# One block for the relative-position attention stage, three turning banks in a ring, and two results in one PSUM bank

## The reference, cut to what matters

```python
b, s, d = x.shape                       # 4, 512, 128
idx = jnp.arange(s)
dist = jnp.clip(idx[None, :] - idx[:, None], -R, R) + R          # R = 64
pe_k, pe_v = rel_emb_k[dist], rel_emb_v[dist]                    # (s, s, 8)
qkv = jnp.transpose((x @ W_qkv + b_qkv).reshape(b, s, 3, H, hd), (2, 0, 3, 1, 4))
q, k, v = (qkv[0], qkv[1], qkv[2])
q = q / jnp.sqrt(jnp.asarray(hd, x.dtype))
score = jnp.einsum('bhqd,bhkd->bhqk', q, k) + jnp.einsum('bhqd,qkd->bhqk', q, pe_k)
attn = jax.nn.softmax(score, axis=-1)
ctx = jnp.einsum('bhqk,bhkd->bhqd', attn, v) + jnp.einsum('bhqk,qkd->bhqd', attn, pe_v)
return jnp.transpose(ctx, (0, 2, 1, 3)).reshape(b, s, d) @ W_out + b_out
```

## Time and profile before

| | |
|---|---|
| Times of three runs | 1484.61, 1489.88, 1497.74 us; median 1489.88 |
| The profiled execution | 1488.59 us; its span, from the first to the last instruction, 1486.9 us |
| PE busy | 1159.3 us (78%) |
| DVE busy | 839.2 us (56%) |
| ACT busy | 712.7 us (48%) |
| POOL busy | 306.2 us (21%) |
| Mean granted TensorE clock | 0.906 |

### The profile page before, as it was taken

The page is one execution under the profiler, slowest core; times in us unless marked ns, Lnnn a source line. Parts: engine busy times, 40 slices in busy tenths (PEclk is TensorE's granted clock), DMA queues, the critical chain, the costliest instruction groups (busy, mean ns, idle before and its releaser), DMA issues. The chain is left out here.

```text
span 1486.9 us, 35646 instructions
## 1 busy us (share of the span) xinstructions
PE 1159.3 (78%) x14780; PEld 578.3 (39%) x14780; DVE 839.2 (56%) x1359; ACT 712.7 (48%) x1328; POOL 306.2 (21%) x639
## 2 busy tenths in 40 slices
PE   5677677888858997578999999999676655588886
PEld 2222332333233442246666666666443223122221
DVE  3575336777632323237666666666226342799994
ACT  4100443777522223536665665555232332389894
POOL 1443010333202322034223223222002101100000
PEclk9999866999968998689999999999889886699998
DMA  4000006111005320140030030110200000611100
GB/s 163 1 0 0 1 0 213 46 46 46 3 0 115 70 44 0 72 72 4 3 24 4 3 24 3 10 11 3 17 1 0 0 1 1 214 36 47 36 24 30
DMA packets 133665, 51.61 MB, mean 35 GB/s; under 512 B 103113, under 2 KB 125657, under 8 KB 132858
## 3 DMA queue, kind: packets, MB, share of 16 engines
q1 hardware_dynamic: 133506, 49.34, 14.3%
HBM read 33.12 MB, written 15.81 MB: 33 GB/s over the span
## 5 line engine op out<-in xcount | busy, mean ns | idle before, releaser
L1728 DVE TENSOR_REDUCE re_nmax<-ps 128x1 f32<-128x512 f32 x256 | 158.9, 683 | 113.1 <-PE ps L1562 113.1
L1577 PE MATMUL ps<-const,re_p 128*128 128x128 f32 x1024 | 154.8, 284 | 33.0 <-DVE re_pT L1743 26.6
L1695 ACT ACTIVATE re_p<-ps,re_nmax 128x512 f32<-128x512 f32 x256 | 154.5, 693 | 16.2 <-DVE re_nmax L1728 16.2
L850 DVE TENSOR_REDUCE ga_nmax<-ps 128x2 f32<-128x1024 f32 x128 | 147.9, 1217 | 14.3 <-PE ps L656 14.2
L1684 ACT ACTIVATE re_pT<-ps 128x512 f32<-128x512 f32 x128 | 76.6, 598 | 162.0 <-PE ps L1577 162.0
L783 ACT ACTIVATE ga_pt<-ps 128x512 f32<-128x512 f32 x256 | 139.2, 598 | 30.6 <-PE ps L691 28.9
L1577 PEld LDWEIGHTS ps<-const,re_p 128*128 128x128 f32 x1024 | 109.1, 142 | 63.4 <-ACT re_p L1695 47.2
L850 DVE TENSOR_REDUCE da_nmax<-ps 128x2 f32<-128x256 f32 (+3 forms) x128 | 102.3, 822 | 38.3 <-PE ps L667 36.9
L783 ACT ACTIVATE da_pt<-ps 128x512 f32<-128x512 f32 (+3 forms) x256 | 97.5, 438 | 46.6 <-PE ps L691 45.6
L1743 DVE COPY re_pT<-ps 128x512 f32<-128x512 f32 x128 | 82.6, 686 | 22.9 <-PE ps L1577 22.2
L710 PE MATMUL ps<-ga_pt,ga_v 128*9 128x256 f32 x1024 | 81.1, 385 | 9.6 <-ACT ga_osum L796 9.4
(11 more groups left out here) (384 smaller groups left out, 2020.9 us busy)
## 6 DMA issues: line engine op xcount, KB each, us to landing
ex_gates<-gates_scratch SPq DMA_DIRECT2D x4, 2048.0 KB, 14.7
da_stacks<-da_qkparts SPq DMA_DIRECT2D x8, 384.0 KB, 3.1
da_qst<-da_stacks SPq DMA_DIRECT2D x32, 96.0 KB, 2.3
da_kst<-da_stacks SPq DMA_DIRECT2D x32, 96.0 KB, 2.4
ga_stacks<-ga_qkparts SPq DMA_DIRECT2D x8, 384.0 KB, 3.1
ga_qst<-ga_stacks SPq DMA_DIRECT2D x32, 96.0 KB
ga_kst<-ga_stacks SPq DMA_DIRECT2D x32, 96.0 KB
da_stacks<-da_qkparts SPq DMA_DIRECT2D x8, 256.0 KB, 3.1
```

Of the source, the lines that this page charges most:

```text
L850: nc.vector.tensor_reduce(nmax[:, u % 2, :, pr, qt], g.ps[:, score_bank[step]:score_bank[step] + 2, 0:keys_of(qt)], AX.X, ALU.max, negate= ...
L1577: last = nc.tensor.transpose(g.ps[:, T_BANK + tile % 2, bass.ts(kt, 128)], p[:, QUAD_ORDER[idx], bass.ts(kt, 128)], g.c("ident"))
L1695: nc.scalar.activation(p[:, quad, :], g.ps[:, S_BANK + quad, :], ACT.Exp, bias=nmax[:, s % 2, idx:idx + 1]).then_inc(exped, 1)
L1728: nc.vector.tensor_reduce(nmax[:, s % 2, idx:idx + 1], g.ps[:, S_BANK + quad, :], AX.X, ALU.max, negate=True).then_inc(maxed, 1)
```

## The change

- The block of projections and the block of the attention become one. TensorE projects batch by batch and swaps each batch's queries right after it, with banks 0 to 5 for the projections in turns and 6 and 7 for the swaps. SP stores each batch's queries as they come and loads the first two batches back at once. Before its first scores TensorE waits for all of the copies, the tables (`less`), and the bias. The buffers of the projections (`xn`, `q_tok`, `zero`, `raw`) now lie in the second half of `pT`, so engines wait for the stores and the tables before they first write there (step 4).
- The banks for turned tiles are three (4, 5, 6), used as a ring; the pieces of a batch's tail take their turn in the same ring.
- Bank 7 holds the far unit in columns 0 to 127 and the near values in the next 64. ScalarE copies each after every step (`copy_values`, `copy_near`); both groups of matmuls wait for the other's copy. VectorE masks the near values out of SBUF (`near`), one step later than before and behind its copies of tiles.
- TensorE turns all four tiles before the next step's scores. ScalarE takes its four exponentials first, and then copies tiles 2 and 3.
- The far unit runs four steps late; the logarithm of the tail stands between the second and third exponentials, its exponential at the end of the step.
- The near values are stored and fetched back for each group of four steps (a quarter of a batch); for the quarter that ends a batch, the loads of the queries two batches on go ahead of its fetches.

The diff, cut to its core:

```diff
-    FAR_LAG = GS + 1
-    TAIL_LAG = STEPS_B + 2 * GS - 3
-    S_BANK, T_BANK, V_BANK, N_BANK = 0, 4, 6, 7
+    FAR_LAG = GS
+    TAIL_LAG = STEPS_B + GS
+    S_BANK, T_BANK, T_BANKS, V_BANK = 0, 4, 3, 7
...
+        ring = []
+        for step in range(ALL_STEPS):
+            ring += [("tail", phase, tail_batch(step, phase)) for phase in range(3)
+                     if tail_batch(step, phase) is not None]
+            if step < NSTEPS:
+                ring += [("tile", step, idx) for idx in range(4)]
+        slot_of = {entry: n for n, entry in enumerate(ring)}
...
+        def bank_of(*entry):
+            return T_BANK + slot_of[entry] % T_BANKS
...
+        far_out = g.ps[:, V_BANK, 0:128]
+        near_out = g.ps[:, V_BANK, 128:128 + 2 * HD * OCT]
...
+                pe.wait_ge(g.weights_loaded[5], 16)
+                for b in range(B):
+                    project(b)
+                    swap(b)
...
+                pe.wait_ge(copied, 3 * B)
+                pe.wait_ge(bias_added, 1)
+                pe.wait_ge(less, 2 * OCT + 2)
...
+                def wait_ring(slot):
+                    if slot < T_BANKS:
+                        return
+                    what, n, m = ring[slot - T_BANKS]
+                    if what == "tail":
+                        pe.wait_ge((logged, divided, added)[n], m + 1)
+                    elif m < 2:
+                        pe.wait_ge(dve_pT, 2 * n + m + 1)
+                    else:
+                        pe.wait_ge(act_pT, 2 * n + m - 1)
...
                     if s >= 1:
-                        pe.wait_ge(masked, s)
...
+                        pe.wait_ge(near_out_read, s)
...
-                        if n >= 1:
-                            pe.wait_ge(osum_out, n)
+                    pe.wait_ge(near_out_read, min(unit + FAR_LAG - 1, NSTEPS))
+                    if unit >= 1:
+                        pe.wait_ge(osum_out, unit)
...
                 for s in range(ALL_STEPS):
                     if s < NSTEPS:
                         score(s)
-                    if 1 <= s <= NSTEPS:
-                        turn(s - 1, 3)
                     if FAR_LAG <= s < NSTEPS + FAR_LAG:
                         far_unit(s - FAR_LAG)
                     if 1 <= s <= NSTEPS:
                         near_values(s - 1)
+                    tail(s)
                     if s < NSTEPS:
-                        for idx in range(3):
+                        for idx in range(4):
                             turn(s, idx)
-                    tail(s)
...
+                def copy_near(s):
+                    if s >= 2:
+                        act.wait_ge(o_done, s - 1)
+                    nc.scalar.activation(near[:, s % 2, :], near_out, ACT.Identity).then_inc(near_out_read, 1)
...
+                def copy_values(unit):
+                    n, quad = divmod(unit, GS)
+                    b, qt = divmod(n, QT)
+                    act.wait_ge(far_done, unit + 1)
+                    if b >= 2 and unit % STEPS_B == 0:
+                        act.wait_ge(joined, b - 1)
+                    nc.scalar.activation(osum[:, b % 2, quad, bass.ts(qt, 128)], far_out, ACT.Identity)\
+                        .then_inc(osum_out, 1)
...
                 for s in range(ALL_STEPS):
-                    if 1 <= s <= NSTEPS:
-                        evacuate(s - 1, 3)
                     if s < NSTEPS:
...
+                        exponentials(s, 0)
+                        exponentials(s, 1)
...
+                        nc.scalar.activation(inverse[:, :], g.ps[:, bank_of("tail", 0, b), :], ACT.Ln)\
+                            .then_inc(logged, 1)
+                    if s < NSTEPS:
+                        exponentials(s, 2)
+                        exponentials(s, 3)
+                        evacuate(s, 2)
+                        evacuate(s, 3)
+                    if 1 <= s <= NSTEPS:
+                        act.wait_ge(near_done, s)
+                    if FAR_LAG <= s < NSTEPS + FAR_LAG:
+                        copy_values(s - FAR_LAG)
+                    if 1 <= s <= NSTEPS:
+                        copy_near(s - 1)
...
                 for b in range(B):
...
+                    sp.wait_ge(q_out, b + 1)
+                    sp.dma_start(q_dram[b * T:(b + 1) * T, :].rearrange("(t p) c -> p t c", p=128),
+                                 q_tok[:, b, :, :]).then_inc(q_stored, 16)
+                    if b < 2:
+                        sp.wait_ge(q_stored, 16 * (b + 1))
+                        load_queries(b)
+                sp.wait_ge(q_stored, 16 * B)
+                for n in range(GROUPS):
+                    b, qt = divmod(n, QT)
+                    sp.wait_ge(o_done, GS * (n + 1))
+                    octets = slice(16 * qt, 16 * qt + 16)
+                    sp.dma_start(o_dram[b, octets].rearrange("a p d -> p a d"), o[:, b % 2, octets, :])\
+                        .then_inc(o_stored, 16)
+                    sp.wait_ge(o_stored, 16 * (n + 1))
+                    if qt == QT - 1 and b + 2 < B:
+                        load_queries(b + 2)
...
+                    for two in range(2):
+                        sp.dma_start(ot[64 * two:64 * two + 64, qt, :].rearrange("p (h d) -> p h d", d=HD),
+                                     rows[two]).then_inc(ot_loaded, 16)
```

More of the change, by code:

```diff
@@ L1500, in far_values @@
                             .then_inc(far_ready, 1)
+                nc.gpsimd.memset(ends[:, :, :], 0.0).then_inc(set_up, 1)
+                nc.gpsimd.memset(v9[:, :, :, HD:HD + 1], 1.0).then_inc(set_up, 1)
+                nc.gpsimd.memset(zero, 0.0).then_inc(set_up, 1)
+                pool.wait_ge(copied, 2)
                 set_keys(0)
@@ L1654, in tail @@
                         pe.wait_ge(divided, b + 1)
-                        pe.wait_ge(masked, min(step, NSTEPS))
-                        nc.tensor.matmul(g.ps[:, N_BANK, :], g.w("aout"), oT[:, :], start=True, stop=True)\
-                            .then_inc(made, 1)
+                        wait_ring(slot_of["tail", 2, b])
+                        nc.tensor.matmul(g.ps[:, bank_of("tail", 2, b), :], g.w("aout"), oT[:, :], start=True,
+                                         stop=True).then_inc(made, 1)
                 for s in range(ALL_STEPS):
@@ L1679, in free_pT, with exponentials @@
                         act.wait_ge(near_done, GS * (n - 1))
+                def exponentials(s, idx):
+                    act.wait_ge(maxed, 4 * s + idx + 1)
+                    if s >= 1:
+                        act.wait_ge(turned, 4 * (s - 1) + idx + 1)
+                    nc.scalar.activation(p[:, QUAD_ORDER[idx], :], g.ps[:, S_BANK + QUAD_ORDER[idx], :], ACT.Exp,
+                                         bias=nmax[:, s % 2, idx:idx + 1]).then_inc(exped, 1)
                 def evacuate(s, idx):
@@ new lines, in _ @@
+                table = ins["rel_v"]
+                for to, n, at in ((0, 128, T - 128), (128, 64, T - 256 + 64), (192, 64, T)):
+                    overlapping = bass.AP(table.tensor, at * HD, [[HD, 128], [1, n * HD]])
+                    sp.dma_start(rel_v[:, to:to + n, :].rearrange("p s d -> p (s d)"), overlapping)\
+                        .then_inc(v_table, 16)
+                sp.wait_ge(set_up, 1)
+                for n, row in ((0, 0), (1, table.shape[0] - 1)):
+                    one_row = bass.AP(table.tensor, row * HD, [[0, 128], [1, HD]])
+                    sp.dma_start(ends[:, n, 0:HD], one_row).then_inc(ends_loaded, 16)
```

331 lines of the change are left out of this document (140 added, 191 removed).

## The result

| | before | after |
|---|---|---|
| Median of 4 runs each | 1489.29 us (1484.61 to 1497.74) | 1440.79 us (1439.25 to 1450.89) |
| Ratio, 95% interval | | 0.968 (0.962 to 0.975) |
| Way in | 36.30 | 25.84 |
| Loop, 62 periods | 386.67 | 362.93 |
| Way out | 30.90 | 18.58 |

The last four lines are cut as in the prediction: from the start of the block to the second step's first row maximum, on to the last step's first maximum, and to the end of the addition to x. The forecast was 1443 us in a range of 1430 to 1466. The three parts give 46.5 us of gain against 46.9 booked. The profiled execution of after is the longest of its four (1450.89); outside the stage, where nothing was changed, it lost 8.8 us against that of before (1488.59 - 1450.89 = 37.7, and 46.5 - 37.7 = 8.8). Its mean granted clock was 0.904, that of the other three 0.915 to 0.917.

A forecast was written before the change was run, and what follows sets the result against it. TensorE, busy 91% of the loop, idles mostly on VectorE's copies. Savings of 10.8 (way in), 25.7 (loop), 0 (tails) and 10.4 us (way out) sum to 46.9: 1488.6 becomes 1441.7, as median 1443 us, range 1430 to 1466.

The forecast's parts named there:

- Way in: Stage start to second step's first row maximum: early query load brings second maximum to 652.0, saving 10.8 us, bounds 7 and 12.
- Way out: Last step's maxima to stage end: quarter stores and fetches cut 30.9 to 20.5 us, saving 10.4, bounds 7 and 12.5.
- The third bank removes the wait before the third tile: Middle loop steps: 0.51 us of TensorE idle before the third tile goes, saving 0.45 us a step.
- TensorE becomes the bound: Middle loop steps: TensorE's own work, 5.69 us, exceeds the waits' 5.50, so the step falls from 6.14 to 5.69.
- the loop of waits: Loop: scores to maxima 1.64, maxima through first tile's copy 3.3, last tile 0.56, together 5.50 us in a middle step.
- the 5.6 to 5.8 that were to show it right: Loop: sign that the forecast holds, middle periods between 5.6 and 5.8 us.
- The first rival: Loop: the fourth tile takes the place of the wait it frees, step stays 6.14 us; 1469 us, chance 0.12.
- Edge steps: Loop steps near a batch's ends: the waits decide, 5.72 falls to 5.41 us, saving 0.31 in each of 16.
- Tails at 0: Three pieces ending each batch, in the ring of three: at most +0.4 x 3 = 1.2 us against free banks, booked 0.
- Shared bank: Far and near values in one bank: no cost, 0.28 us of cover; as second rival, late copies give 1459 us, chance 0.12.
- no cold restart: Way in: the first period becomes 5.4 us, with TensorE not restarting cold.
- The clock: Third rival, loop: TensorE granted 1.2 GHz, middle step roughly 10.2 us, half the loop gives 1583 us; chance 0.04.

The follow-up runs named there:

- The square: Kernel after with two or three banks, four tiles ahead of the scores or fourth behind: loops 400.0 and 388.4 us (two banks), 362.9 and 354.4 (three).
- the late load: Against the kernel after, the first two batches' queries loaded only after all four stores, still in one block: 1451.66 us.

## Why the prediction was right, and where its steps were off

**The third bank removes the wait before the third tile, the masking multiply no longer matters.** Right, and the largest term. The square shows 34 to 37 us for it, more than the 25.7 booked for the loop, because another part takes some back. The multiply costs next to nothing in middle steps; ahead of the copies it would cost 0.07 us in an edge step.

**"TensorE becomes the bound", at 5.69 us.** This step failed in its working. The prediction added up two sums, TensorE's list (5.63, taken as 5.69) and the loop of waits that starts at the maxima (5.50), took the larger, and left no wait. The middle step is neither sum but a path that crosses from one to the other. TensorE's groups ahead of the tiles take 3.33 us (812.99 to 816.32); the copy of the first tile starts 0.79 after that tile does and takes 0.69; 0.12 later comes the fourth tile's weight load, and 0.59 later the next scores: together 5.52. The prediction did name this wait ("only the fourth waits for the first tile's copy"), but let the copy start when the maxima end, where it starts when the first tile is ready, and so found no idle time in it.

The list itself was too long. Three tiles in a row take 811.74 - 810.23 = 1.51 us, where 0.56 each makes 1.68: a tile takes 0.56 only as the last before the scores. So the old wait before the third tile was 0.70 us rather than 0.51, and 6.14 - 0.70 = 5.44, the period of the old order with three banks. In the order of the kernel after the list is about 5.28 (an estimate: 3.33, 1.51, and 0.44 for one more tile between two others, as the trace of the old order has it), and some 0.24 of wait make up the rest.

That the forecast of 5.69 lies near the measured 5.52 to 5.59 is in part luck, and the middle periods lie outside the 5.6 to 5.8 that were to show it right. The total for the loop (23.7 against 25.7) hides this. Middle steps gained 0.6 each instead of 0.45, which with the edge steps would make 46 x 0.6 + 16 x 0.31 = 32.6 us. The tails (2.1) and the gaps that no engine released (5.3 more than before, see below) were not booked and took most of the difference back. Two errors of about 7 us cancelled: that is luck.

**The order of tiles.** The first rival put the fourth tile between the last exponential and the next scores, held by "the same copy of the first tile", and gave it 0.12 for the whole gain. The wait for that copy is there, at a third of the size: the order costs 8.5 us of loop. A middle step takes 5.54 instead of 5.44, some 4.6 us in 46 steps, and the gaps without a releaser are 4 us more than in the old order. I had taken four tiles ahead for a part of the gain; the square shows that it is a loss in either column of banks. It is hidden because the third bank's gain is four times as large.

**Edge steps.** 5.41 booked, 5.38 to 5.50 measured, and most of them are decided as booked, by the loop of maxima and exponentials.

**Tails at 0.** Nearly so: the three long steps after the first batch took 7.14, 8.23 and 7.0 us before and take 6.79, 7.90 and 6.58 now, 1.1 less together, while three ordinary steps gained 1.8. Measured so, a tail costs 0.7 more than it did beyond its steps.

**Shared bank.** Right that it costs nothing. The far copy takes 0.27 us (0.28 booked) and the near copy 0.23, and they overlap, so they end at 0.99 instead of 1.27. The cover is 0.65 us where I had 0.28, and the two runs with more copies lie on either side of its end. The Trainium skill's advice in "Perfetto Trace Analysis", section "Matmuls", to rotate independent groups of matmuls through different banks is thus a question of slack here: with one more copy of 0.38 us the step kept its length, and with 1.21 us of them the far unit waited 0.45 us in most middle steps.

**Way in.** 10.8 booked, 10.5 measured in one execution and 9.0 in the other. The chain was right: the loads decide (the late load gives all of it back), and they arrived at 646.37, or 645.3 with this block's later start (1.05 us) taken off, where 644.7 was expected (the 646 that was to show it wrong did not reckon with the later start). What I had ruled out, "no cold restart", happens in the second execution: queries come 0.43 us after TensorE could use them, the clock falls, and the first four tiles take 3.60 us instead of 2.39. It is the more common case: of seven executions with this way in, two took 25.8 us and kept the clock, five took 27.2 to 27.4 and lost it (the same kernel again and four with edits elsewhere).

**Way out.** 10.4 booked, 12.3 measured. The store of a quarter takes 3.0 us where I took 4.1, and from the join to the end 4.9 instead of 6.1, with the clock at 1.00: the wait for the fetches is now 0.73 us, not 10.7, and the output's two matmuls take 1.12 us, not 2.08. The Trainium skill has a rule for DMAs that GpSimd issues ("DMA: Bandwidth & Descriptors", section "Anatomy of one DMA": about 2.0 us and the bytes over 436 GB/s); for 64 KB it would make 2.2 us, an estimate from that page. These stores are issued by SyncE, in 32-byte pieces, and took 3.0 us for a quarter and 9.2 for a whole batch, so they neither bear the rule out nor refute it.

**The clock.** Right: 1.00 through 362.9 us of denser work.

**What I had not booked.** Gaps inside the near values, released by no engine. The profile sums them to 2.5 us in the loop of before, but 2.2 of these are something else: one of 0.73 us in each of three steps at the start, which stands ahead of the group and not in it:

```profile
669.28 0.60 ACT L1684 ACTIVATE re_pT<-ps 128x512 f32<-128x512 f32 x1 [1.69 <-PE ps L1577]
...
669.98 0.45 PE L1602 MATMUL ps<-re_rel_v,re_pT 128*32 128x16 f32 x32 [0.73 <-issue]
```

There no far unit stands between yet, and near values begin 0.10 us after the end of ScalarE's copy of the fourth tile (669.88), for which they wait; in the step before these three the profile itself names that copy. That leaves 0.3 us before, against 5.6 after and 5.3 when run again. Such a step:

```profile
849.70 0.40 PE L1562 MATMUL ps<-re_rel_v,re_pT 128*32 128x16 f32 x26
851.19 0.52 PE L1562 MATMUL ps<-re_rel_v,re_pT 128*32 128x16 f32 x38 [1.09 <-issue]
```

The 64 small matmuls of one group stand still for 1.09 us in their middle. The order of the groups matters most. With the old order the gaps inside near values sum to 0.3 us (before), 1.1 (two banks) and 1.5 to 1.6 (three banks, three builds, in which TensorE waits least of all). With four tiles ahead of the scores they are 3.1 to 7.6 us, with two banks too (4.5), and 0.3 in one run alone, that with three more copies. In the new order the band of keys, the far unit and the near values are 128 small matmuls in a row; in the old one the fourth tile stands among them, and in that one run a wait of 0.45 us. Within the new order the gaps are rarer when the transfers are fewer (2.8 against 4.5 to 4.7 in the same stretch) or larger (3.1 against 5.5 in the loop). What supplies TensorE with instructions is a possible cause, since every such gap ends with nothing released, but no run here shows it. Its cause stays open.

## What to carry to other kernels

When an edit has several parts, make the square of its two main ones: here a third turning bank was worth 34 to 37 us, and the new order of tiles that came with it cost 8.5 to 11.6, which a single before and after could not show. The old order with three banks gives 1435.5 to 1438.4 us in three builds (ratios 0.963 to 0.964), against 1441 to 1443 for the kernel after (0.968); the intervals just overlap, but the loops, 353 to 354 against 363 us, do not. Before calling an engine the bound, do not only compare its own list with the loop of waits: follow the path from one to the other, here TensorE's groups, the first tile's copy, and the tile that needs its bank. And where the profile names one releaser and another ends within 0.1 us of it, look which of the two keeps a constant distance over many steps (here 0.12 us behind the copy).

A result that only has to come back from DRAM early should be stored in pieces as it is made. And a shared bank is free as long as its copies end before the turn of the next matmuls in it: find that time in the timeline, and the cost beyond it is one for one.

## What the runs showed of the hardware beyond what was expected

- The granted clock fell to 0.50 on the way in when TensorE, after some 15 us of full work, waited 0.67 us, then 0.37 to 1.89, then 1.43 (and with the late load 0.67, 8.5 and 1.26). It stayed at 1.00 when the middle wait was 0.22 us or less, and through the way out with several waits of 0.4 to 1.2 us between its groups. Filling the middle wait with useless matmuls kept it at 1.00.
- Dense groups of small matmuls stand still for 0.2 to 1.6 us now and then, with no engine to release them, up to 7.6 us in a loop of some 360. With a group of large ones or a wait among them it was 0.3 to 1.6 us.
- A store of a quarter of a batch took 3.0 to 4.4 us to the transfers issued behind it, that of a whole batch 7.7 to 9.2: two to three times as long, in the same 32-byte pieces.
- TensorE's next weight load began 0.05 us after the end of the exponential it waited for, but 0.12 us after the end of the VectorE copy it waited for.
